# Mamba block with a gated network on one core: order of the transposes, rstd on GpSimd, norms folded into evictions

## The reference

```python
mod = (silu(c) @ wmod).reshape(16, 6, 1, 256)
sa, ca, ga, sb, cb, gb = ...            # six rows for each sequence; ga, gb keep their sign and are at least 0.25 in size
h = layernorm(x) * (1 + ca) + sa
xn = layernorm(h, ln1_w, ln1_b)
x1 = mamba(xn); x2 = flip(mamba2(flip(xn)))
x = x + ga * (layernorm(x1 + x2, ln2_w, ln2_b) + xn)
h = layernorm(x) * (1 + cb) + sb
x = x + gb * ffn(h)                     # silu-gated layer, two 1024x1024 layers with exact gelu, one back to 256

def mamba(x):                           # E = 512 channels, N = 64 states
    xp, z = split(x @ W_in.T)
    xc = silu(conv4(xp) + conv_b)
    dt_lo, B, C = split(xc @ W_xp.T)
    dt = softplus(dt_lo @ W_dt.T + dt_b)
    h[t] = exp(dt[t] * A) * h[t-1] + (dt[t] * xc[t]) * B[t]     # for each channel and state
    y[t] = sum over n of h[t] * C[t]
    return ((y + xc * D) * silu(z)) @ W_out.T
```

## Time and profile before

| what | value |
|---|---|
| median of three runs | 13681.96 us (13680.24 to 13686.08) |
| profiled execution | 13708.09 us, of which the span 13706.3 us |
| VectorE busy | 12472.7 us, 91% |
| GpSimd busy | 11259.0 us, 82% |
| ScalarE busy | 10941.1 us, 80% |
| TensorE busy | 10481.0 us, 76% |
| granted clock of TensorE, mean | 0.862 of full speed |
| HBM traffic | 105 GB/s |

### The profile page before, as it was taken

The page is one execution under the profiler, slowest core; times in us unless marked ns, Lnnn a source line. Parts: engine busy times, 40 slices in busy tenths (PEclk is TensorE's granted clock), DMA queues, the critical chain, the costliest instruction groups (busy, mean ns, idle before and its releaser), DMA issues.

```text
span 13706.3 us, 178924 instructions
## 1 busy us (share of the span) xinstructions
PE 10481.0 (76%) x51212; PEld 5968.3 (44%) x51212; DVE 12472.7 (91%) x7742; ACT 10941.1 (80%) x23356; POOL 11259.0 (82%) x5316
## 2 busy tenths in 40 slices
PE   5667877778787787877777777787877878777776
PEld 2334444444343444444444444443444444444445
DVE  5999999999999999999999999999999999999991
ACT  6788888788787888878888788887878878788882
POOL 4888888888888888888888888888888888888891
PEclk7778888889898898988888898898988889889898
DMA  2223333333233333333323333332333333233232
GB/s 86 83 91 101 108 100 118 106 107 116 93 120 102 114 109 105 114 98 117 117 97 104 104 118 110 102 117 93 119 105 109 117 99 117 98 115 116 98 106 85
DMA packets 601084, 1450.50 MB, mean 106 GB/s; under 512 B 64016, under 2 KB 105120, under 8 KB 595504
## 3 DMA queue, kind: packets, MB, share of 16 engines
q1 hardware_dynamic: 599984, 1437.65, 31.8%
HBM read 1347.12 MB, written 90.28 MB: 105 GB/s over the span
## 4 chain that ended last, share of the span: by engine, by line
PE 26%; issue 23%; ACT 19%; DVE 16%; POOL 14%; DMA 1%; DVEq 0%; POOLq 0%; ACTq 0%; SPq 0%
POOL state L1244 11%; DVE state L1214 9%; PE driven L843 7%; ACT state L1023 6%; ACT v_sb L1036 6%; PE q_ps L798 6%; PE y_ps L857 4%; DVE driven L1203 2%; PE b_ps L833 2%; POOL v_sb L1276 2%; PE q_ps L785 2%; PE p_ps L706 1%; PE p_ps L714 1%; ACT L1023 1%; ACT hid L1006 1%
## 5 line engine op out<-in xcount | busy, mean ns | idle before, releaser
L1244 POOL TENSOR_TENSOR state<-state,c_rep 128x1024 f32<-128x1024 f32 x4096 | 9709.5, 2394 | 2011.9 <-DVE state L1214 2010.4
L1214 DVE TENSOR_TENSOR_SCAN state<-state,driven 128x1024 f32<-128x1024 f32 x4096 | 9104.6, 2271 | 581.8 <-PE driven L843 445.5
L1036 ACT ACTIVATE v_sb<-u_t,b_t 128x128 f32<-128x128 f32 x12288 | 3997.4, 506 | 1711.5 <-PE driven L843 1709.6
L1023 ACT ACTIVATE state<-ud_rep,cols_sb 128x512 f32<-128x512 f32 x8192 | 5191.1, 712 | 6.3 <-PE y_ps L857 3.2
L857 PE MATMUL y_ps<-state,consts_sb 128*32 128x512 f32 x16384 | 2534.4, 691 | 1824.2 <-POOL state L1244 1817.1
L843 PE MATMUL driven<-consts_sb,v_sb 128*128 128x128 f32 x16384 | 2712.2, 325 | 852.6 <-DVE state L1214 842.6
L843 PEld LDWEIGHTS driven<-consts_sb,v_sb 128*128 128x128 f32 x16384 | 2251.1, 168 | 2147.1 <-DVE state L1214 1704.8
L1203 DVE TENSOR_TENSOR driven<-ud_rep,b_ps 128x1024 f32<-128x1024 f32 x2048 | 2391.0, 1214 | 17.1 <-DMA ud_rep<-ud_rows 17.1
L798 PE MATMUL q_ps<-hid,wq_sb 128*128 128x256 f32 x8192 | 2130.4, 406 | 133.9 <-ACT hid L1001 80.0
L798 PEld LDWEIGHTS q_ps<-hid,wq_sb 128*128 128x128 f32 x8192 | 1535.7, 197 | 880.6 <-issue 647.2
L857 PEld LDWEIGHTS y_ps<-state,consts_sb 128*32 128x32 f32 x16384 | 341.5, 114 | 3003.5 <-POOL state L1244 2460.9
(11 more groups left out here) (115 smaller groups left out, 5646.0 us busy)
## 6 DMA issues: line engine op xcount, KB each, us to landing
c_rep<-bc_rows SPq DMA_DIRECT2D x2048, 256.0 KB, 3.0
ud_rep<-ud_rows SPq DMA_DIRECT2D x512, 512.0 KB, 4.1
wq_sb<-in_h SPq DMA_DIRECT2D x512, 512.0 KB, 3.9
wq_sb<-in_f SPq DMA_DIRECT2D x128, 512.0 KB, 4.6
wp_sb<-in_win SPq DMA_DIRECT2D x64, 512.0 KB, 4.6
dt_sb<-conv_taps SPq DMA_DIRECT2D x32, 1024.0 KB, 5.2
ud_rows<-u_pad SPq DMA_DIRECT2D x128, 256.0 KB, 3.4
ud_rows<-dt_sb SPq DMA_DIRECT2D x128, 256.0 KB, 3.4
```

Of the source, the lines that this page charges most:

```text
L1023: ins = act.activation(state[:, unit % STATE_RING, j, :], ud_rep[:, nth % 2, j, 1, :], ACT.Exp, scale=a_neg[:, d, c, j, g:g + 1])
L1036: ins = act.activation(v_sb[:, unit // 2 % V_RING, tt, :, :, n].rearrange("p j e -> p (j e)"), u_t[:, nth % 2, tt, :], ACT.Identity, scale ...
L1214: dve.tensor_tensor_scan(flat, flat, driven[:, q % DRIVE_RING].rearrange("p j t -> p (j t)"), 0.0, ALU.mult, ALU.add).then_inc(scanned, 1)
L1244: pool.tensor_tensor(part, part, c_rep[:, unit % ROW_RING, :].unsqueeze(1).to_broadcast([P, 2, T]), ALU.mult).then_inc(was_read, 1)
```

## The change

Four edits that belong together:

1. TensorE, for an odd unit u+1: the transposes of half 0 now stand ahead of the sum over n of unit u-1, those of half 1 behind it. Where unit u begins a pass of 16 (`ends_pass`), the old order stays.
2. rstd goes from ScalarE to GpSimd: seven instructions on 128x4 elements (variance + eps, to the power -0.5, and a Newton step), each waiting for the one before. The Newton step leaves VectorE.
3. The h norm's scale and shift (ln1) go into ScalarE's evictions of T0 and T1, the n norm's into those of N0 and N1, as a scale and bias for each partition; the setup makes the needed columns (`mod_cols`) with eight small matmuls. The o norm's scale is multiplied into the gate in the setup. The mix becomes: gate * ln2_w times the normed o (mix0), added to x (mix1); GpSimd makes x + gate * ln2_b + gate * ln1_b + gate * ln1_w * xn beforehand in three instructions on 128x1024 (pre0 to pre2, units 7 to 9). The xn that is stored is the one without scale and shift. The x norm stays as it was.
4. Softplus: each eviction of v becomes two, Relu into `dt_sb` and Abs into `u_sb`, both from PSUM; the step "abs" goes; 1 + u moves from step 16 to step 15; L1189 becomes a plain add.

```diff
-    act += [(s + 15, part, "abs", 1), (s + 15, part, "exp", 1), (s + 16, part, "one", 1)]
+    act += [(s + 15, part, "exp", 1), (s + 15, part, "one", 1)]
...
-    dve = [(s, part, name + "_stats", TT), (s + 1, part, name + "_aggr", TT), (s + 3, part, name + "_norm", 4 + TT),
-           (s + 4, part, name + "_scale", 1), (s + 5, part, name + "_shift", 1)]
-    return [(s + 2, part, name + "_rstd", 2)], dve
+    dve = [(s, part, name + "_stats", TT), (s + 1, part, name + "_aggr", TT), (s + 3, part, name + "_norm", TT)]
+    if name == "x":
+        dve += [(s + 4, part, "x_scale", 1), (s + 5, part, "x_shift", 1)]
+    return [(s + 2, part, name + "_rstd", 7)], dve
...
-    dve += [(MIX_AT + i, "early", f"mix{i}", 1) for i in range(3)]
+    pool += [(Q_AT + i, "early", f"pre{i}", 1) for i in range(3)]
+    dve += [(MIX_AT + i, "early", f"mix{i}", 1) for i in range(2)]
...
+                    to_drive, ends_pass = scans and unit + 1 in PE_UNITS, unit % NG == 0
+                    if to_drive and not ends_pass:
+                        drive(at, unit + 1, 0)
                     if before_scans or scans and unit:
                         accumulate(at, unit - 1)
-                    if scans and unit + 1 in PE_UNITS:
+                    if to_drive and ends_pass:
                         drive(at, unit + 1, 0)
+                    if to_drive:
                         drive(at, unit + 1, 1)
...
-                        act.activation(dt_sb[:, m, :], p_ps[:], ACT.Identity, bias=dt_b[:, d, m:m + 1]).then_inc(done, 1)
+                        act.activation(dt_sb[:, m, :], p_ps[:], ACT.Relu, bias=dt_b[:, d, m:m + 1]).then_inc(done, 1)
+                        act.activation(u_sb[:, m, :], p_ps[:], ACT.Abs, bias=dt_b[:, d, m:m + 1]).then_inc(done, 1)
...
-                        emit(dve.scalar_tensor_tensor(t, v, EPS, r, ALU.add, ALU.mult), True)
-                        emit(dve.tensor_tensor(t, t, r, ALU.mult), True)
-                        emit(dve.tensor_scalar(t, t, -0.5, 1.5, ALU.mult, ALU.add), True)
-                        emit(dve.tensor_tensor(r, r, t, ALU.mult), True)
...
-                        emit(dve.scalar_tensor_tensor(dt_sb[:], dt_sb[:], 0.0, sz_sb[d][:], ALU.max, ALU.add),
-                             True)
+                        emit(dve.tensor_tensor(dt_sb[:], dt_sb[:], sz_sb[d][:], ALU.add), True)
...
+                    pool.wait_ge(dve_side.sem, dve_side.done(at, part, name[0] + "_aggr"))
+                    v, r, t, ve = mv[:, i, :, 1], rstd[:, i, :], newton[:, i, :], stats[:, i, :, 1]
+                    emit(pool.tensor_tensor(ve, v, eps.to_broadcast([P, TT]), ALU.add))
+                    emit(pool.tensor_tensor(r, ve, less_half.to_broadcast([P, TT]), ALU.pow))
+                    emit(pool.tensor_tensor(t, r, r, ALU.mult))
+                    emit(pool.tensor_tensor(t, t, ve, ALU.mult))
+                    emit(pool.tensor_tensor(t, three.to_broadcast([P, TT]), t, ALU.subtract))
+                    emit(pool.tensor_tensor(r, r, half.to_broadcast([P, TT]), ALU.mult))
+                    emit(pool.tensor_tensor(r, r, t, ALU.mult))
...
+                    if name == "pre0":
+                        pool.wait_ge(q_in.sem, q_in.done(at, "early", "q"))
+                        pool.tensor_tensor(xn_q[:], xn_q[:], over_tiles(mod_q[:, 1, :]), ALU.mult).then_inc(done, 1)
+                    elif name == "pre1":
+                        pool.tensor_tensor(x_q[:], x_q[:], over_tiles(mod_q[:, 2, :]), ALU.add).then_inc(done, 1)
+                    else:
+                        pool.wait_ge(done, pool_side.done(at, part, "pre1"))
+                        pool.tensor_tensor(x_q[:], x_q[:], xn_q[:], ALU.add).then_inc(done, 1)
```

121 lines of the change are left out of this document (71 added, 50 removed).

## The result

The changed kernel took 13443.2 us (median of 4 runs, 13442.3 to 13446.0), the kernel before beside it 13684.0: a ratio of 0.982, interval 0.981 to 0.983, so 241 us faster. Forecast were 13185 us, 498 us faster. The time lies inside the range; the gain, 241 of 498 us, is a little under half of what was forecast. Later comparisons ran beside the kernel before at 13689.2, 13687.2 and 13689.3, so that times can be set side by side within some 5 us.

What follows compares the result with a forecast made beforehand. VectorE's in-order queue was taken as the bound. Gains of 169 + 24 + 160 + 85 + 60 = 498 us from the profiled 13708.1 left 13210, less 26.1 for the median of runs: 13185, range 12940 to 13480.

Steps and rivals of the forecast that it cites:

- rstd: Newton step and its wait leave VectorE, 209.6 us, less 50 of waits for GpSimd: gain 160 us.
- The chain: Seven dependent four-element GpSimd instructions making rstd, taken as c = 2.2 us, with 50 us of VectorE waits in all.
- The slack: Time before the norms in which GpSimd's rstd instructions would cost VectorE nothing: 7.55 us a pass, 0.85 at unit 11.
- The norms' scale and shift: Three quarters of VectorE's 225.9 us go into ScalarE's existing evictions at no cost: gain 169 us.
- the mix: Two VectorE instructions for three, GpSimd making three products in exchange: gain 24 us, between 0 and 68.
- Softplus: VectorE's waits for ScalarE at units 40 and 108 shrink: gain 85 us, bounds 50 and 135.
- The wait at unit 108: VectorE's 6.76 us wait for ScalarE at softplus goes; 3.5 us a pass gained, 52 us in 15 passes.
- The transposes: One half ahead of TensorE's sum shortens scans' waits: net gain 60 us, bounds -50 and +170.
- The loss at the low clock: TensorE's sum between the halves delays second scans at eleven units, up to 1.5 us each, 10.5 us a pass.
- (b): Rival, chance 0.15: GpSimd's rstd instructions take c = 8, waits 399 us in all for 50: 13535 us.
- (a): Rival, chance 0.18: TensorE's new order gives nothing or loses, -50 for +60: 13295 us.

Runs made afterwards that it cites:

- the cut chain: The changed kernel with GpSimd's rstd chain cut to the addition and the power, refinement left out: 13342.8 us, ratio 0.975.
- both runs on the order: TensorE's new order alone in the kernel before: 13555.4 us; the changed kernel with TensorE's old order put back: 13509.1 us.
- the measuring part: Nine forms of VectorE instruction on constant data, alone and beside GpSimd products, ahead of the kernel before; run once, norm's form 0.41 us alone, 2.42 beside products.

## Why the prediction was wrong, point by point

**rstd: the step that failed.** The prediction costed the edit as 109 and 101 that go and 50 that come: a gain of 160. Alone it lost 71 us, and within the change 99. The chain was sized well (about 2.7 us for 2.2; the wait for it 44 for 50). The mistake is in what stands behind it. The sum has no term for the norm instruction itself, L1152: its 88 us were taken as its own price, to be kept, and any rise was put at nothing. They were its price in a gap that the Newton instruction in front of it had opened: that one, four elements and 829 ns on average, was where the product in flight was paid. I had written the rule down for it, "its own work plus the rest of one GpSimd product", for instructions with two SBUF operands. I did not ask who would pay once it was gone. The norm has one tensor operand and a mean of 410 ns, so it did not look like an instruction that waits. The slack was wrong as well: I called the time from 4352.53, when GpSimd was through with its `v_sb`, to 4355.48 free for the chain. It was not: GpSimd began the two products of unit 11 at 4352.49 and was busy with them to 4357.15. A chain put there pushes them back, onto the norm. With the norm on VectorE the chain's length is paid in full, as the cut chain shows (100 us for 96); with the norm on ScalarE it is not (34).

Put the other way round: without this step the forecast's sum is 498 - 160 = 338, or 13344 us. The kernel with rstd moved back took 13344.0. That the two agree so closely is in part luck, since two of the other terms were off in opposite directions.

**The norms' scale and shift, the mix.** 169 and 24 forecast; 168.8 and 32.6 in the rows of VectorE's busy time. This edit was not run alone. The evictions that took the scale and shift over were costed at nothing; they take 0.78 us where they took 0.59, some 17 us of ScalarE in all, for which no run shows the price.

**Softplus.** 85 forecast, 56 alone, and 32 by the rows of the changed kernel (waits -109 and +35, L1197 +63, L1203 -20). The wait at unit 108 fell from 6.76 to 1.80, where the forecast had it gone. Too small was the price of arriving early: an instruction that waited for ScalarE found GpSimd idle, and one that doesn't wait meets products. At unit 108 the step took 3.05 us for 2.29, and at unit 40, where its wait of 2.39 is gone, 6.38 for 2.43: more was lost there than the wait had cost. It is the same mistake as with rstd, in small. Neither Relu nor Abs brought a load of a function table in its evictions, and no row shows a loss of that kind.

**The transposes.** 60 forecast, 134 alone, 66 within the change. The waits themselves were not near 385, they were 246: the order removes more waiting than I had counted, and 70 to 86 us of it come back as waits for ScalarE, which the prediction said it had not counted. The loss at the low clock was smaller than costed. At unit 10 the first half and the sum again ran at the lower level (1.97 and 1.92 us, granted clock 0.50 to 0.52), but the second half took 1.10 at a granted clock of 1.00, and the second scan of the next unit waited 0.58, not over 1:

```profile
4287.67 1.92 PE L871 MATMUL y_ps<-state,consts_sb 128*32 128x512 f32 x8
```

```profile
4290.66 2.29 DVE L1227 TENSOR_TENSOR_SCAN state<-state,driven 128x1024 f32<-128x1024 f32 x1 [0.58 <-PE driven L857]
```

At TensorE's unit 38, where the scans had waited 3.83 us, the changed kernel has a wait of 0.38 before the second scan:

```profile
4475.19 2.29 DVE L1227 TENSOR_TENSOR_SCAN state<-state,driven 128x1024 f32<-128x1024 f32 x1 [0.38 <-PE driven L857]
```

**The terms don't add up exactly.** Order 134, softplus 56, norms and mix 201 by their rows, rstd -71: together 320, measured 241. With the order's gain and rstd's loss as they are inside the change, 66 and -99, the sum is 224, or 17 short of the 241: several edits fill the same waits. How this is split between the softplus edit, never undone inside the change, and the norms, never run alone, was not tried.

**The rivals.** (b) came closest in time, by another route: it had the chain long, c = 8, with the price in the wait for it. What cost was not the wait, but the busy time of the instruction behind it. (a) is refuted by both runs on the order.

## What to carry to other kernels

An instruction of VectorE that looks too long for its size may be paying for a product on GpSimd, as the first Newton instruction did here. When it went, the next one of a form that is held up paid instead; what moved to ScalarE was really gone, and a form with a PSUM operand was not held up in the measuring part. Before work is moved to GpSimd, ask what GpSimd owes at that moment, and what VectorE will stand at while GpSimd works it off.
